# Parts of two tiles moved from VectorE to GpSimd, one tile normalised earlier, and 21 unread matmuls

## The reference

```python
x = x + tanh(g_xattn) * attention(layernorm(x), ctx, ctx, gamma)       # 8 "heads" of 8 rows per unit
h = layernorm(x)
qx = round(clip(h * s)) / s            # s = 127 / max|h| of the row
a, b = qx @ qw_gate.T, qx @ qw_up.T    # weights rounded to -1, 0, 1 times a scale
h = silu(a) * b                        # 1024 wide
h = ln_weight * h * rsqrt(mean(h * h) + 1e-6)
x = x + tanh(g_ffn) * (quantised(h) @ qw_down.T)
```

## Time and profile before

| | us |
|---|---|
| median of 3 runs | 201.59 (201.09 to 202.09) |
| the profiled execution | 199.28 |
| its span, first to last instruction | 197.5 |
| busy: PE / PEld | 142.9 / 82.1 |
| busy: DVE | 161.5 (82%) |
| busy: ACT | 121.8 |
| busy: POOL | 140.4 |

### The profile page before, as it was taken

One profiled execution on the slowest core, in us unless ns is written; L12 is line 12 of the kernel. 1 busy time (PEld: TensorE's weight loads), 2 busy tenths in 40 slices (PEclk: granted clock), 3 DMA queues, 4 the chain that ended last, 5 costly groups with the idle time before them and its releaser, 6 DMA issues.

```text
span 197.5 us, 3861 instructions
## 1 busy us (share of the span) xinstructions
PE 142.9 (72%) x1270; PEld 82.1 (42%) x1270; DVE 161.5 (82%) x292; ACT 121.8 (62%) x245; POOL 140.4 (71%) x263
## 2 busy tenths in 40 slices
PE   0008339996588869889868898999999897529343
PEld 0005126563254446345335564754545544314122
DVE  7989985779958979689699977999845967988971
ACT  4414107786545748578588759879868874373730
POOL 6878379534929998779989887889887887841010
PEclk9999955899999999999999999999999999985855
DMA  4688966569975725673271163230110000100000
GB/s 127 192 238 261 284 189 245 200 214 375 279 204 188 263 60 157 218 215 108 78 238 40 41 192 108 63 83 28 35 56 1 3 27 0 33 0 28 0 24 29
DMA packets 19936, 25.31 MB, mean 128 GB/s; under 512 B 4146, under 2 KB 17202, under 8 KB 18514
## 3 DMA queue, kind: packets, MB, share of 16 engines
q1 hardware_dynamic: 19172, 20.80, 34.1%
q10 hardware_dynamic: 744, 4.26, 6.2%
HBM read 17.93 MB, written 6.91 MB: 126 GB/s over the span
## 4 chain that ended last, share of the span: by engine, by line
POOL 40%; PE 16%; DVE 15%; DMA 12%; issue 9%; SPq 4%; ACT 3%; POOLq 0%; DVEq 0%; ACTq 0%
POOL wf L634 5%; PE sr L1319 4%; DMA qs<-mp 4%; POOL vw L550 4%; PE ob L1333 4%; DMA scr_q<-qp 3%; PE sr L1299 3%; POOL wf L662 3%; POOL wf L664 3%; DVE mx L975 3%; DVE wf L1066 2%; DVE kh L1056 2%; POOL wf L647 2%; POOL wt L666 2%; PE sr L1407 2%
## 5 line engine op out<-in xcount | busy, mean ns | idle before, releaser
L975 DVE TENSOR_REDUCE mx<-sr 128x2 f32<-128x512 f32 x128 | 82.0, 680 | 12.4 <-PE sr L1299 11.9
L757 ACT ACTIVATE pr<-sr 128x512 f32<-128x512 f32 x128 | 70.5, 597 | 13.2 <-PE sr L1319 12.5
L1299 PE MATMUL sr<-ks,qs 128*128 128x256 bf16 x256 | 50.6, 293 | 19.9 <-DMA qs<-scr_q 14.5
L1319 PE MATMUL sr<-qs,ks 128*128 128x256 bf16 x256 | 50.1, 282 | 8.1 <-DVE mx L975 3.8
L1299 PEld LDWEIGHTS sr<-ks,qs 128*128 128x128 bf16 x256 | 23.2, 104 | 37.9 <-issue 18.2
L1333 PE MATMUL ob<-pr,vw 128*32 128x256 f32 x512 | 34.3, 385 | 1.0 <-ACT osb L773 0.8
L1319 PEld LDWEIGHTS sr<-qs,ks 128*128 128x128 bf16 x256 | 22.6, 100 | 18.5 <-DVE mx L975 5.8
L1333 PEld LDWEIGHTS ob<-pr,vw 128*32 128x32 f32 x512 | 13.5, 109 | 13.4 <-ACT pr L757 5.0
L1373 PE MATMUL sr<-wt,xt 128*128 128x512 bf16 x64 | 17.9, 411 | 0.2 <-DVE xt L1150 0.2
L797 ACT ACTIVATE kh<-sr,ghs 128x512 f32<-128x512 f32 x16 | 11.0, 688 | 8.9 <-PE sr L1373 8.7
L550 POOL TENSOR_SCALAR vw<-vt,cx 128x128 f32<-128x128 f32 x16 | 9.7, 613 | 7.6 <-DMA vt<-in_vt 3.9
(11 more groups left out here) (123 smaller groups left out, 239.5 us busy)
## 6 DMA issues: line engine op xcount, KB each, us to landing
qs<-scr_q SPq DMA_DIRECT2D x7, 576.0 KB
ks<-scr_k SPq DMA_DIRECT2D x7, 576.0 KB
scr_k<-kp SPq DMA_DIRECT2D x8, 192.0 KB, 3.9
scr_q<-qp SPq DMA_DIRECT2D x8, 192.0 KB, 3.7
scr_o<-osb SPq DMA_DIRECT2D x12, 128.0 KB, 5.1
scr_k<-kp SPq DMA_DIRECT2D x8, 128.0 KB, 4.7
wf<-in_wg ACTq DMA_DIRECT2D x1, 1024.0 KB, 7.1
wf<-in_wu ACTq DMA_DIRECT2D x1, 1024.0 KB, 8.4
```

The lines of the kernel that those rows point to most:

```text
L757: nc.scalar.activation(pr[:, b % PR_BUFS, m % 4, :], bank("score", m)[:, :], ACT.Exp, scale=float(DH) ** -0.5).then_inc(exp_done, 1)
L975: nc.vector.tensor_reduce(mx[:, h % 2, 2 * at:2 * at + 2], bank("max", n)[:, :].rearrange("p (c n) -> p c n", c=KC), axis=AX.X, op=ALU.max ...
L1299: mm = nc.tensor.matmul(bank("max", n)[:, c * COLS:(c + 1) * COLS], qs[:, t % STACKS, at:at + P], ks[:, t % STACKS, u * COLS:(u + 1) * COL ...
L1319: mm = nc.tensor.matmul(bank("score", m)[:, c * COLS:(c + 1) * COLS], ks[:, t % STACKS, at:at + P], qs[:, t % STACKS, u * COLS:(u + 1) * C ...
```

## The change

- `late_weigh` for tiles 6 and 7 is split: the low half of y is made by GpSimd (`late_weigh_low`, at the step of `z0`), the high half and both maxima stay with VectorE, now all behind `z1`.
- For tile 6 (`POOL_HIGH`) the rounding of y's high half and its conversion to bf16 go from VectorE to GpSimd (`round_high`).
- Tile 7: GpSimd's root (`rstd`) is done at step 173, between the scale of tile 5 and its rounding, which became a function of its own, `round_y`. On ScalarE `int_x` and `copy_x` of tile 7 come at steps 175 and 176, ahead of `copy_ht` of tile 5. `gu0` and `gu1` of tile 7 come at 193 and 194, so that `down` of tile 5 lies between them.
- ScalarE takes `tanh1` and `sq0` of tile 6 ahead of `int_y` of tile 5, and `tanh1` of tile 7 behind `int_low` of tile 6. `result` of tile 5 goes behind `z0` of tile 7.
- `stay_busy`: 21 matmuls of 128 x 512 (bf16) into `ob`, whose results nobody reads: 11 ahead of step 177's work, 1 ahead of 192's, 5 ahead of 212's, 4 ahead of 245's.

```diff
+POOL_HIGH = [6]
+    "rstd": [None, None, None, None, None, None, None, 173],
+    "scales": [None, None, None, None, None, None, None, 183],
-    "int_x": [69, 76, 97, 110, 124, 139, 162, 181],
+    "int_x": [69, 76, 97, 110, 124, 139, 162, 175],
-    "copy_x": [70, 79, 99, 112, 127, 142, 170, 192],
-    "gu0": [72, 83, 100, 116, 129, 144, 168, 203],
+    "copy_x": [70, 79, 99, 112, 127, 142, 170, 176],
+    "gu0": [72, 83, 100, 116, 129, 144, 168, 193],
-    "gu1": [77, 86, 104, 117, 130, 145, 173, 204],
-    "tanh1": [77, 86, 105, 117, 131, 145, 175, 201],
+    "gu1": [77, 86, 104, 117, 130, 145, 173, 194],
+    "tanh1": [77, 86, 105, 117, 131, 145, 172, 203],
-    "sq0": [None, None, None, None, None, None, 180, 218],
+    "sq0": [None, None, None, None, None, None, 173, 218],
-    "copy_h": [98, 106, 124, 136, 158, 175, 208, 268],
+    "copy_h": [98, 106, 124, 136, 158, 177, 208, 268],
-    "result": [102, 112, 127, 140, 172, 185, 233, 299],
+    "result": [102, 112, 127, 140, 172, 205, 233, 299],
+BUSY_AT = {177: 11, 192: 1, 212: 5, 245: 4}
...
+            def late_weigh_low(t):
+
+                pool.wait_ge(y_int, t - 1)
+                pool.wait_ge(z_done, 2 * t + 1)
+                nc.gpsimd.tensor_tensor(y[:, t % 2, 0:512], z[:, t % 2, 0:512], lnw[:, 0:512], ALU.mult).then_inc(y_low, 1)
+
+            def round_high(t):
+
+                i = t - LATE
+                pool.wait_ge(y_step, LATE + 6 * i + 5)
+                nc.gpsimd.tensor_scalar(y[:, t % 2, 512:INNER], y[:, t % 2, 512:INNER], col(sh, t), ROUND, ALU.mult, ALU.add).then_inc(yr_high, 1)
+                pool.wait_ge(yr_high, i + 1)
+                if i >= 1:
+                    pool.wait_ge(high_turned, i)
+                else:
+                    pool.wait_ge(h_turned, LATE)
+                nc.gpsimd.tensor_scalar(yi[:, 512:INNER], y[:, t % 2, 512:INNER], -ROUND, 1.0, ALU.add, ALU.mult).then_inc(yi_high, 1)
...
+                t = due("rstd", n)
+                if t is not None:
+                    rstd_x(t)
+                t = due("scale_y", n)
+                if t is not None and t < LATE:
+                    round_y(t)
+                t = due("z0", n)
+                if t is not None and t >= LATE:
+                    late_weigh_low(t)
...
+            def late_weigh(t):
+
+                i = t - LATE
+                high = slice(512, INNER)
                 if i == 0:
                     dve.wait_ge(lnw_in, DMA)
+                dve.wait_ge(y_int, t - 1)
+                dve.wait_ge(z_done, 2 * t + 2)
+                nc.vector.tensor_tensor(y[:, t % 2, high], z[:, t % 2, high], lnw[:, high], ALU.mult).then_inc(y_half, 1)
+                dve.wait_ge(y_low, i + 1)
+                nc.vector.tensor_reduce(ym2[:, t, 0:1], y[:, t % 2, 0:512], axis=AX.X, op=ALU.max,
+                                        apply_absolute_value=True).then_inc(ym_half, 1)
+                late_var(t)
                 dve.wait_ge(y_half, i + 1)
+                nc.vector.tensor_reduce(ym2[:, t, 1:2], y[:, t % 2, high], axis=AX.X, op=ALU.max,
                                         apply_absolute_value=True).then_inc(ym_half, 1)
...
+            def stay_busy(count):
+
+                pe.wait_ge(o_copied, 2 * TILES)
+                for _ in range(count):
+                    nc.tensor.matmul(ob[:, :, :].rearrange("p r n -> p (r n)"), identb[:, :], wgt[:, 0, 0:512], start=True, stop=True)
+
             pe.wait_ge(consts, 2)
             for n in range(STEPS):
+                if n in BUSY_AT:
+                    stay_busy(BUSY_AT[n])
```

More of the change, by code:

```diff
@@ L283, in build @@
         y_scaled = sem("y_scaled"); y_int = sem("y_int")
-        sq_half = sem("sq_half"); y_half = sem("y_half"); ym_half = sem("ym_half"); y_var = sem("y_var"); y_rstd = sem("y_rstd")
+        sq_half = sem("sq_half"); y_low = sem("y_low"); y_half = sem("y_half"); ym_half = sem("ym_half"); y_var = sem("y_var"); y_rstd = sem("y_rstd")
         y_step = sem("y_step"); yr_low = sem("yr_low"); yr_high = sem("yr_high"); yi_low = sem("yi_low"); yi_high = sem("yi_high")
@@ L646, in scale_y, with round_y @@
                 step(nc.gpsimd.tensor_scalar(col(sh, t), col(rc, t), col(fh, t), QMAX, ALU.mult, ALU.mult))
+            def round_y(t):
                 nc.gpsimd.tensor_scalar(y[:, t % 2, :], y[:, t % 2, :], col(sh, t), ROUND, ALU.mult, ALU.add).then_inc(y_scaled, 1)
@@ L698, in _ @@
                         norm_x(t)
-                    else:
-                        rstd_x(t)
-                        late_scales_x(t)
+                t = due("scales", n)
+                if t is not None:
+                    late_scales_x(t)
                 t = due("scale_x", n)
@@ L715, in _ @@
                         rstd_y(t)
+                        if t in POOL_HIGH:
+                            round_high(t)
+                t = due("rstd", n)
+                if t is not None:
+                    rstd_x(t)
[5 more added lines that the diff above has]
+                    late_weigh_low(t)
         @block.scalar
@@ L1064, in gate_up @@
                         dve.wait_ge(sq_half, 2 * (t - 1 - LATE))
-                        dve.wait_ge(y_half, 2 * (t - 1 - LATE))
+                        dve.wait_ge(y_low, t - 1 - LATE)
+                        dve.wait_ge(y_half, t - 1 - LATE)
                 nc.vector.tensor_tensor(z[:, t % 2, half], up[:, :], th[:, h, :], ALU.mult).then_inc(z_done, 1)
-            def late_weigh(t, h):
-                half = slice(h * 512, (h + 1) * 512)
-                i = 2 * (t - LATE) + h
+            def late_weigh(t):
+                i = t - LATE
+                high = slice(512, INNER)
                 if i == 0:
                     dve.wait_ge(lnw_in, DMA)
[L1074 to L1083, removed]
+                dve.wait_ge(y_int, t - 1)
[5 more added lines that the diff above has]
+                late_var(t)
                 dve.wait_ge(y_half, i + 1)
-                nc.vector.tensor_reduce(ym2[:, t, h:h + 1], y[:, t % 2, half], axis=AX.X, op=ALU.max,
+                nc.vector.tensor_reduce(ym2[:, t, 1:2], y[:, t % 2, high], axis=AX.X, op=ALU.max,
                                         apply_absolute_value=True).then_inc(ym_half, 1)
@@ L1121, in late_scale_y @@
                 step(nc.vector.tensor_scalar(col(sh), col(rc), col(fh), None, ALU.mult))
-                nc.vector.tensor_scalar(y[:, t % 2, 512:INNER], y[:, t % 2, 512:INNER], col(sh), ROUND, ALU.mult, ALU.add).then_inc(yr_high, 1)
+                if t not in POOL_HIGH:
+                    nc.vector.tensor_scalar(y[:, t % 2, 512:INNER], y[:, t % 2, 512:INNER], col(sh), ROUND, ALU.mult, ALU.add).then_inc(yr_high, 1)
                 step(nc.vector.tensor_scalar(col(osc), col(ah), cd[:, 0:1], None, ALU.mult))
+                if t in POOL_HIGH:
+                    return
                 dve.wait_ge(yr_high, i + 1)
@@ L1232, in _ @@
                         gate_up(t, h)
-                        if t >= LATE:
-                            late_weigh(t, h)
+                        if t >= LATE and h == 1:
+                            late_weigh(t)
                 t = due("max_y", n)
```

## The result

The changed kernel takes 199.31 us (median of 19 runs), the kernel before 201.59 (19 runs); the medians are 2.28 us apart. Some executions of either kernel are several us longer than its shortest, so the ratio on record, 0.9851 with a 95% interval from 0.9813 to 0.989, compares only the fast ones of each. That is a gain of 3.0 us (2.2 to 3.8), where I had forecast 1.0 with a range that held 199.31. The profiled execution of the changed kernel took 204.33 us (span 202.5), and its extra time lies ahead of the part that was changed. The row from which the two programs can be compared is GpSimd's weighing of tile 5, which stands ahead of everything that was changed.

The account below looks back on a forecast made before the run. VectorE's order of work sets the end, the clock only where TensorE's result is awaited. Terms sum to 1.82 us, less 0.84 for the last fillers = 0.98 us, set against 201.59: 200.6 us; range 198.7 to 201.9.

Parts of the forecast that it names:

- rival 1: TensorE's clock is full at the end of the kernel: gain 2.9 us, 198.7 us; chance 0.25 including the weaker form.
- VectorE's walk: VectorE's new order of work followed through the profiled execution's last 26 us: lead over the old order 1.82 us.
- the last fillers and half the clock to the end: Behind tile 6's down product, four half-clock fillers of 0.45 us delay the last transposes: 0.84 us off the gain.
- The two blockings: VectorE's normalising and rounding of tile 7 are held up under GpSimd's instructions: 0.55 and 0.47 us off the lead.
- Rivals 3 and 4: 3: GpSimd and VectorE pass without blocking, 200.1 us, chance 0.08. 4: GpSimd's half weighing near 2.36 us eats lead, 201.6, 0.08.
- The half weighing at 1.28 us: GpSimd's new 512-wide weighing of tile 6's low half takes 1.28 us, with bounds 0.73 and 2.36.
- Rounding of tile 6 off VectorE, 1.04 us: Rounding and conversion of tile 6's high half, moved to GpSimd, add 1.04 us to VectorE's lead.
- The fillers in the middle, nothing on the path: The fillers ahead of the last four cost nothing at full clock; tile 7's products are done before anyone asks.
- Rival 2: The eleven fillers do not hold the clock, VectorE waits 1.7 us for tile 7's squares: slower, 202.3 us; chance 0.12.
- rival 1 in its weaker form: Only the last products of TensorE have the full clock: gain 1.8 us, 199.8 us; chance 0.25 together with rival 1.

Follow-up runs that it names:

- low weighing later: Changed kernel with GpSimd's weighing of tile 6's low half behind tile 7's three small values, not ahead of them: tail 27.58 us, ratio to the kernel before 0.9909.
- no fillers: Changed kernel with none of the 21 filler matmuls: tail 28.17 us, ratio to the kernel before 0.9872.
- before plus fillers: Kernel before the change with only the 21 filler matmuls added: tail 30.20 us, ratio to the kernel before 0.994.
- The second execution: Changed kernel itself, nothing altered, profiled a second time: tail 28.61 us against 27.80 us at the first.
- gap filled: Changed kernel with its last four fillers replaced by eleven between the halves of tile 6's down product: tail 27.86 us, ratio to the kernel before 0.9866.

## Why the prediction was off

The direction was right, and the time fell into a range that was made wide enough for rival 1; the size was a third of what was measured (0.98 us against 2.68 in the tail, 1.0 against 3.0 timed). Two terms of the sum failed: VectorE's walk, put at 1.82 us and measured at 2.43, and the 0.84 us taken off for the last fillers and half the clock to the end, where the end gave 0.25 us. By its own steps:

- *The two blockings* (0.55 and 0.47 us): the mechanism was right, 0.14 and 0.16 us behind GpSimd's ends as forecast. As prices, the first was 0.70 us (1.11 against 0.41, begun 0.13 us sooner than I had it) and the second 0.31 (0.66 against 0.35); taking the second away brought 0.30 us (low weighing later). Rivals 3 and 4 are out.
- *The half weighing at 1.28 us:* measured 1.26.
- *VectorE's walk, 1.82 us:* mis-sized, it is 2.43. Where tile 6's second half starts I was 0.23 us late, at tile 6's variance 0.35, at tile 7's halves 0.30 and 0.49, at tile 7's variance 0.63. The first 0.13 us are there at the start: tile 7's normalising begins at 8.57 us of the tail, and I had 8.70. What is added behind it is in the main one habit: I set each instruction behind the recorded end of the last, whereas the next often starts 0.06 to 0.11 us ahead of it (182.95 against 183.03 in the fence above). That is so on ScalarE too, where the chain to tile 6's second square (copy, transpose, copy, copy, square) took 2.70 us, and I had 2.91. The two short waits for ScalarE that I had put in (0.1 us for that square, less for tile 7's second tanh) do not show in the trace.
- *Rounding of tile 6 off VectorE, 1.04 us:* 0.76 when it is given back.
- *The fillers in the middle, nothing on the path:* right from both sides, 0.11 us (no fillers) and 0.04 us (before plus fillers). Rival 2 is out: the clock held, and where it did not, without fillers, nothing was behind them.
- *The last four fillers and half the clock to the end, 0.84 us off the gain:* this is the larger of the two failed steps. The fillers took 0.55 us, but in the first execution the clock came back for the last products, which gave 0.83. That is rival 1 in its weaker form (a chance of 0.25 together with the full one): 2.43 - 0.55 - 0.03 + 0.83 = 2.68 us, where 0.03 was lost between the transposes and the products. The second execution had my case, half the clock to the end, with 30.48 - 28.61 = 1.87 us; there the term was 0.54 us and not 0.84. So even where the clock did as I forecast, the gain was nearly twice my 0.98. Which of the two came was chance. If the kernel before keeps its 30.48 (one execution), the tails over many executions would give something between 1.87 and 2.68; the timed 3.0 has its lower end at 2.2.

So of the missing 1.7 us in the first profiled execution, 0.6 are VectorE's walk and 1.1 the end (0.3 the fillers' price, 0.8 the clock). Which of the two ends is the more frequent was not settled; nor was the large difference between executions ahead of the changed part explained.

## What to carry to other kernels

Moving work off the busiest engine and reordering the engine that feeds it are worth little apart (0.15 and 0.69 us) and much together (2.43): what the one saves alone turns into a wait for the other. Matmuls that only keep the clock up can pay only where TensorE's result is awaited at once; in the middle of this tail 17 of them bought 0.1 us. At the end, the one kernel that kept the full clock had its fillers over before the real input stood and no idle stretch of TensorE above 0.56 us in the last 8 us; the one with idle stretches of 1.06 and 1.37 us there (gap filled) lost it. Four fillers directly ahead of awaited work, after a fall, cost 0.55 us in six executions of seven, and the clock came back in time to repay them in three. When executions differ by more than the change, measure from the last row that both programs share.

## What was not expected of the hardware

The same program, twice, had its last eight products at 1.03 and at 1.82 us, since the clock came back at 26 and at 28.5 us of the tail, with the same work ahead. An instruction of VectorE that is blocked by GpSimd does not run its whole time behind GpSimd's end: 256 elements issued under GpSimd ended 0.14 to 0.16 us behind it (0.35 to 0.41 us when free), and 512 with two SBUF inputs 0.55 us behind (180.71 + 0.89 against 179.78 + 1.27; 0.69 us when free). So 0.14 to 0.27 us of the instruction's own time pass during the wait. Whether that is its start-up was not measured.
